# Symmetric normalised adjacency with residual layer norm: four of forty gate products go to GpSimd, and two rows are added at a time

## The reference, cut to what matters

```python
# x: (8, 2048, 64), W = adj: (8, 2048, 2048), U: (2048, 16), all float32
Ws = 0.5 * (W + swapaxes(W, -1, -2))
A = sigmoid(U @ U.T)                      # the gate: symmetric, the same for all batches
K = Ws * A[None]
d = rsqrt(maximum(K.sum(axis=-1), 1e-12))
K = K * d[:, :, None] * d[:, None, :]
x = layernorm(x + w_scale * einsum('bnm,bmc->bnc', K, x))
```

## Time and profile before

| | |
|---|---|
| median of three runs | 469.59 us |
| the profiled execution | 466.65 us |
| its span, first to last instruction | 464.8 us |
| TensorE busy | 436.6 us, 94% |
| VectorE busy | 416.3 us, 90% |
| ScalarE busy | 208.4 us, 45% |
| GpSimd busy | 113.4 us, 24% |
| moved by DMA | 143.11 MB, mean 308 GB/s |
| mean granted TensorE clock | 0.988 |

### The profile page before, as it was taken

How to read it: one execution, slowest core, us unless ns; L and a number is a source line. 1 busy time by engine, 2 the same in 40 slices (tenths; PEclk the granted TensorE clock), 3 DMA queues, 4 the chain that set the end, 5 groups by cost and what they waited for, 6 DMA issues and landing times.

```text
span 464.8 us, 14448 instructions
## 1 busy us (share of the span) xinstructions
PE 436.6 (94%) x5318; PEld 232.5 (50%) x5318; DVE 416.3 (90%) x1154; ACT 208.4 (45%) x655; POOL 113.4 (24%) x133
## 2 busy tenths in 40 slices
PE   7888999999999999989999899989999899999893
PEld 6556444554455543555445544565445543564351
DVE  6988868999899998999899998999899999999645
ACT  3797432554255442554335533463426542554320
POOL 0000000022520334103340235103340225203443
PEclk9997999999999999999999999999999999999998
DMA  8999699988999799997999898998989998994012
GB/s 285 388 327 381 240 383 329 355 314 305 333 365 321 280 364 315 373 339 272 361 336 356 295 362 302 391 335 298 383 308 355 333 328 309 385 334 179 2 45 47
DMA packets 101387, 143.11 MB, mean 308 GB/s; under 512 B 35824, under 2 KB 35824, under 8 KB 101360
## 3 DMA queue, kind: packets, MB, share of 16 engines
q1 hardware_dynamic: 86496, 139.01, 84.4%
q10 hardware_dynamic: 14864, 3.74, 3.7%
HBM read 138.54 MB, written 4.19 MB: 307 GB/s over the span
## 4 chain that ended last, share of the span: by engine, by line
PE 67%; DVE 15%; issue 7%; ACT 5%; DMA 4%; POOL 0%; DVEq 0%; POOLq 0%; ACTq 0%; SPq 0%
PE yp L442 39%; PE kt L400 12%; PE tw L400 11%; DVE k L671 7%; DVE k L682 5%; ACT k L564 3%; DMA k<-in_adj_dram 3%; PE yp L540 3%; ACT gate L551 2%; PE yp L475 1%; DVE z L702 1%; DMA h<-in_L_gnn_U_dram 1%; DVE deg_parts L682 1%; PE kt L486 1%; PE kt L540 0%
## 5 line engine op out<-in xcount | busy, mean ns | idle before, releaser
L564 ACT ACTIVATE k<-kt 128x512 f32<-128x512 f32 (+3 forms) x288 | 149.2, 523 | 213.8 <-PE kt L400 213.7
L442 PE MATMUL yp<-k,z 128*64 128x512 f32 x944 | 233.2, 607 | 4.3 <-DVE z L702 3.9
L671 DVE TENSOR_TENSOR k<-tw,k 128x512 f32<-128x512 f32 (+2 forms) x320 | 193.0, 603 | 19.8 <-PE tw L400 15.7
L682 DVE CUSTOM_DVE_ANT_0 k<-k,gate 128x512 f32<-128x512 f32 (+2 forms) x320 | 198.7, 621 | 0.0
L400 PEld LDWEIGHTS kt<-ident,k 64*128 64x128 f32 x1920 | 74.3, 140 | 93.4 <-issue 74.5
L400 PEld LDWEIGHTS tw<-ident,k 64*128 64x128 f32 x2176 | 82.6, 140 | 43.9 <-issue 38.5
L400 PE MATMUL kt<-ident,k 64*128 64x64 f32 x1920 | 93.9, 231 | 10.6 <-ACT k L564 9.1
L400 PE MATMUL tw<-ident,k 64*128 64x64 f32 x2176 | 99.0, 228 | 1.5 <-DVE k L671 1.0
L442 PEld LDWEIGHTS yp<-k,z 128*64 128x64 f32 x944 | 55.8, 136 | 69.3 <-issue 54.7
L327 POOL TENSOR_TENSOR d<-deg,minus_half 128x4 f32<-128x4 f32 x32 | 32.4, 1014 | 206.8 <-DVE deg L692 206.2
L564 ACT ACTIVATION_READ_ACCUMULATOR k<-kt 128x1 f32 x288 | 57.2, 199 | 0.0
(11 more groups left out here) (53 smaller groups left out, 140.4 us busy)
## 6 DMA issues: line engine op xcount, KB each, us to landing
k<-in_adj_dram SPq DMA_DIRECT2D x128, 1024.0 KB, 7.3
xt<-in_x_dram ACTq DMA_DIRECT2D x7, 512.0 KB, 8.0
out_dram<-h SPq DMA_DIRECT2D x7, 512.0 KB, 8.4
xt<-in_x_dram SPq DMA_DIRECT2D x1, 512.0 KB, 14.0
out_dram<-k SPq DMA_DIRECT2D x2, 128.0 KB, 2.1
out_dram<-k SPq DMA_DIRECT2D x3, 64.0 KB, 1.7
h<-in_L_gnn_U_dram SPq DMA_DIRECT2D x1, 128.0 KB, 3.4
out_dram<-k ACTq DMA_DIRECT2D x1, 64.0 KB, 1.9
```

The lines of the kernel that those rows point to most:

```text
L442: t = pe.matmul(yp[at:at + C, m // 2, :], z[:, n * G + c, :], K[(n, m)][:, c, :], start=(q == first_unit[m] and c == 0), stop=(q == last_u ...
L564: nc.scalar.activation(K[(j, i)][:, r, c0:UW].rearrange("p (c h e) -> p c h e", h=2, e=H), whole_rows(kt[:, 0:2, :], r % 2, (UW - c0) // P ...
L671: nc.vector.tensor_tensor(row, whole_rows(tw[:, tw_bank[g] // 2 * 2:tw_bank[g] // 2 * 2 + 2, :], g % 2, w // P), row, ALU.add).then_inc(su ...
L682: nc.vector.tensor_tensor_reduce(row, row, A[:, A_AT[g]:A_AT[g] + w], 1.0, 0.0, ALU.mult, ALU.add, deg_parts[:, i * G + r, j:j + 1]).then_ ...
```

## The change

GpSimd makes the gate product of rows 3, 12, 22 and 33 (`POOL_ROWS`; three are 512 wide, row 33 is 256 wide) as a plain product without a row sum. ScalarE takes the row sum of each of these four rows by an extra copy into a scrap tile, four rows later in its own list (`SUM_LAG`). VectorE leaves these rows out and makes 36 gate products. In the six steps off the diagonal VectorE adds two rows by one instruction of 1024 elements (`add_two_rows`), so 24 adds become 12. TensorE's upper transposes wait for a second semaphore (`pool_lower_done`), and the degree sums wait for `row_summed`. The load order of the next batch is changed in two places, and the rows at which the later steps stand are moved, most by one to four rows, `COPY_ROWS[0]` by seven.

```diff
-LOADS = [(0, 1), (0, 0), (0, 2), (0, 3), (1, 0), (1, 1), (1, 2), (2, 0), (1, 3), (3, 0), ...]
+LOADS = [(0, 0), (0, 1), (0, 2), (0, 3), (1, 0), (1, 1), (1, 2), (1, 3), (2, 0), (3, 0), ...]
+POOL_ROWS = [3, 12, 22, 33]
+NP, ND = len(POOL_ROWS), NL - len(POOL_ROWS)
+SUM_LAG = 4
-PRODUCT_ROWS = [29, 29, 32, 32, 33, 33, 35, 35, 38, 38, 39, 39, 42, 44, 44, 45, 45, 45, 46, 46, 46, 47, 50, 50, 52, 54, 56, 56, 58, 60, 62, 64]
-DEG_ROWS = [25, 32, 40, 43]
-Z_ROWS = [26, 35, 43, 44]
-KEEP_ROW = 55
-SCALE_ROW = 50
-COPY_ROWS = [55, 65]
-Y_ROWS = [66, 68]
-Y_SCALE_ROWS = [66, 69]
-ADD_ROWS = [68, 69, 69, 73]
-MEAN_ROW = 76
-CENTER_ROWS = [77, 79, 80, 82]
+PRODUCT_ROWS = [30, 30, 32, 32, 33, 33, 35, 35, 38, 38, 39, 39, 42, 44, 44, 45, 45, 45, 45, 47, 47, 47, 50, 50, 52, 54, 56, 56, 59, 59, 61, 63]
+DEG_ROWS = [25, 32, 42, 42]
+Z_ROWS = [26, 34, 42, 43]
+KEEP_ROW = 59
+SCALE_ROW = 47
+COPY_ROWS = [48, 63]
+Y_ROWS = [63, 68]
+Y_SCALE_ROWS = [63, 68]
+ADD_ROWS = [67, 68, 68, 74]
+MEAN_ROW = 75
+CENTER_ROWS = [75, 77, 78, 78]
...
-VAR_ROW = 84
-DIVIDE_ROWS = [87, 89, 91, 94]
+VAR_ROW = 83
+DIVIDE_ROWS = [85, 87, 88, 91]

 # GpSimd
+            def gate_product(b, g, first):
+                s, r = LOWER[g]
+                w = lower_width(s, r)
+                row = K[STEPS[s]][:, r, 0:w]
+                if first:
+                    pool.wait_ge(gate_ready, g + 1)
+                pool.wait_ge(sum_done, b * NL + (g + 1))
+                nc.gpsimd.tensor_tensor(row, row, A[:, A_AT[g]:A_AT[g] + w], ALU.mult).then_inc(pool_lower_done, 1)

 # TensorE, transpose_rows
-                    pe.wait_ge(lower_done, b * NL + G * (s + 1))
+                    pe.wait_ge(lower_done, b * ND + vector_rows_of(G * (s + 1)))
+                    if POOL_ROWS[0] < G * (s + 1):
+                        pe.wait_ge(pool_lower_done, b * NP + pool_rows_of(G * (s + 1)))

 # ScalarE
+            def row_sum(b, g):
+                s, r = LOWER[g]
+                i, j = STEPS[s]
+                w = lower_width(s, r)
+                act.wait_ge(pool_lower_done, b * NP + (POOL_ROWS.index(g) + 1))
+                nc.scalar.activation(scrap[:, 0:w], K[(i, j)][:, r, 0:w], ACT.Copy,
+                                     accum_out=deg_parts[:, i * G + r, j:j + 1]).then_inc(row_summed, 1)
+                    if row - SUM_LAG in POOL_ROWS:
+                        row_sum(b, row - SUM_LAG)

 # VectorE
+            def add_two_rows(b, g):
+                s, r = LOWER[g]
+                rows = K[STEPS[s]][:, r:r + 2, :].rearrange("p r (c h e) -> p (r c) h e", h=2, e=H)
+                if r == 0:
+                    dve.wait_ge(loaded[STEPS[s]], b * 16 + 16)
+                dve.wait_ge(tw_done, b * NL + (g + 2))
+                pair = tw[:, tw_bank[g] // 2 * 2:tw_bank[g] // 2 * 2 + 2, :].rearrange("p h (c e) -> p c h e", e=H)
+                nc.vector.tensor_tensor(rows, pair, rows, ALU.add).then_inc(sum_done, 2)

 # VectorE, sum_degrees
+                dve.wait_ge(row_summed, b * NP + pool_rows_of(G * (top + 1)))

 # VectorE, steps
-                    add_row(b, g)
+                    if STEPS[g // G][0] == STEPS[g // G][1]:
+                        add_row(b, g)
+                    elif g % 2 == 0:
+                        add_two_rows(b, g)
```

More of the change, by code:

```diff
@@ L39 @@
 LAST_PAIR_OF_BANK = [max(q for q, pair in enumerate(PAIRS) if pair[0][1] // 2 == k) for k in range(2)]
-LOADS = [(0, 1), (0, 0), (0, 2), (0, 3), (1, 0), (1, 1), (1, 2), (2, 0), (1, 3), (3, 0), (2, 1), (3, 1), (2, 3), (3, 2), (2, 2), (3, 3)]
+LOADS = [(0, 0), (0, 1), (0, 2), (0, 3), (1, 0), (1, 1), (1, 2), (1, 3), (2, 0), (3, 0), (2, 1), (3, 1), (2, 3), (3, 2), (2, 2), (3, 3)]
 STORE_AFTER = (3, 1)
@@ L60, with pool_rows_of, vector_rows_of @@
 UPPERS_TO = [sum(upper_rows(t) for t in range(s + 1)) for s in range(len(STEPS))]
+POOL_ROWS = [3, 12, 22, 33]
+NP, ND = len(POOL_ROWS), NL - len(POOL_ROWS)
+SUM_LAG = 4
+def pool_rows_of(n):
+    return sum(g < n for g in POOL_ROWS)
+def vector_rows_of(n):
+    return n - pool_rows_of(n)
 A_AT = [sum(lower_width(*g) for g in LOWER[:n]) for n in range(NL + 1)]
 UPPER_LAG = 2
-PRODUCT_ROWS = [29, 29, 32, 32, 33, 33, 35, 35, 38, 38, 39, 39, 42, 44, 44, 45, 45, 45, 46, 46, 46, 47, 50, 50, 52, 54, 56, 56, 58, 60, 62, 64]
-DEG_ROWS = [25, 32, 40, 43]
-Z_ROWS = [26, 35, 43, 44]
-KEEP_ROW = 55
-SCALE_ROW = 50
-COPY_ROWS = [55, 65]
-Y_ROWS = [66, 68]
-Y_SCALE_ROWS = [66, 69]
-ADD_ROWS = [68, 69, 69, 73]
-MEAN_ROW = 76
-CENTER_ROWS = [77, 79, 80, 82]
+PRODUCT_ROWS = [30, 30, 32, 32, 33, 33, 35, 35, 38, 38, 39, 39, 42, 44, 44, 45, 45, 45, 45, 47, 47, 47, 50, 50, 52, 54, 56, 56, 59, 59, 61, 63]
[9 more added lines that the diff above has]
+CENTER_ROWS = [75, 77, 78, 78]
 SQUARE_ROW = 83
-VAR_ROW = 84
-DIVIDE_ROWS = [87, 89, 91, 94]
+VAR_ROW = 83
+DIVIDE_ROWS = [85, 87, 88, 91]
 LN_PARTS = 4
@@ L151, in bass_graph_resnorm_kernel @@
         rstd = sb("rstd", [P, NC])
+        scrap = sb("scrap", [P, UW])
         ws = sb("ws", [P, 1])
@@ L219, in bass_graph_resnorm_kernel @@
         banks_taken = sem("banks_taken")
+        pool_taken, pool_lower_done, row_summed = sem("pool_taken"), sem("pool_lower_done"), sem("row_summed")
         deg_summed, deg_ready, d_ready, z_ready = sem("deg_summed"), sem("deg_ready"), sem("d_ready"), sem("z_ready")
@@ L327, in degrees @@
                 nc.gpsimd.tensor_tensor(d[:, s], deg[:, s], minus_half[:, s], ALU.pow).then_inc(d_ready, 1)
+            def gate_product(b, g, first):
[6 more added lines that the diff above has]
+                nc.gpsimd.tensor_tensor(row, row, A[:, A_AT[g]:A_AT[g] + w], ALU.mult).then_inc(pool_lower_done, 1)
             def beside_row(b, row):
-                pool.wait_ge(lower_done, b * NL + row)
+                pool.wait_ge(lower_done, b * ND + vector_rows_of(row))
             def beside(b, row, lag):
@@ L351, in steps @@
                 for row in range(NL):
+                    if row in POOL_ROWS:
+                        gate_product(b, row, lags == 1)
                     for lag in range(lags - 1, -1, -1):
@@ L683, in gate_product, with gate_row_product @@
                                                deg_parts[:, i * G + r, j:j + 1]).then_inc(lower_done, 1)
+            def gate_row_product(b, g, first):
+                if g not in POOL_ROWS:
+                    gate_product(b, g, first)
             def sum_degrees(b, k):
                 n0, n1, top = Z_GROUPS[k]
-                dve.wait_ge(lower_done, b * NL + G * (top + 1))
+                dve.wait_ge(lower_done, b * ND + vector_rows_of(G * (top + 1)))
+                dve.wait_ge(row_summed, b * NP + pool_rows_of(G * (top + 1)))
                 dve.wait_ge(upper_done, b * NU + UPPERS_TO[top])
@@ L759, in steps @@
                     if g:
-                        gate_product(b, g - 1, lags == 1)
+                        gate_row_product(b, g - 1, lags == 1)
                     elif lags > 1:
-                        gate_product(b - 1, NL - 1, lags == 2)
+                        gate_row_product(b - 1, NL - 1, lags == 2)
                     for lag in range(lags - 1, -1, -1):
@@ L833, in _ @@
                 steps(b, 3)
-            gate_product(B - 1, NL - 1, False)
+            gate_row_product(B - 1, NL - 1, False)
             for k in range(NZ):
```

## The result

The changed kernel takes 474.13 us (median of 20 runs, 472.05 to 478.80) where the kernel before, run beside it, takes 470.37 (20 runs, 465.13 to 476.11). The ratio, made from pairs on the same chip, is 1.0127 [1.0094, 1.0159]: slower by 1.3%, where the forecast was faster by 1.2%. Ratios leave out the executions that ran disturbed, and medians take in all of them (two of these were as long as 594 and 1002 us), so a ratio is not the quotient of two medians. The profiled execution took 473.46 us with a span of 471.3, against 466.65 and 464.8.

The account below looks back on a forecast made before the run. TensorE was taken as the bound, VectorE close behind. Start +0.7, turn one -0.6, turns two and three -1.5 and -2.0, four late turns -2.4 gave -5.8: from 469.6 to 463.8 us, range 454 to 473.

Parts of the forecast that it names:

- rival A: Whole kernel: VectorE is the real pacer and TensorE's modelled ends hide it; 444 to 452 us, chance 0.10.
- D: VectorE's adds: the two-row pattern streams no faster, so the merge does nothing; 465 us, chance counted within the forecast's 0.55.
- Rival C: At row 46: GpSimd's product of row 3 comes late for TensorE's transposes; 472 to 479 us, chance 0.13.
- rival B: At rows 26 to 28: the gain is eaten where x, load (3,2) and z meet; 466 to 469 us, chance 0.22.
- Where the stall goes: Walk of VectorE and TensorE through rows 24 to 30: about 1.25 us of TensorE idle, a turn of 52.2.
- the early turns: Turns two and three, 54.2 us after a late load, were to gain 1.5 and 2.0, down to 52.2.
- Queues passed: Reordered loads: units only fill earlier, (2,0) keeps about 6.5 us, x just fits; cost 0 to 1 us a turn.
- the start: First batch: ScalarE's row sums at rows 7 and 16 delay kt copies; +0.7 us taken, +1.2 at most.
- Four of them cost nothing: ScalarE's four row sums, 0.6 to 0.8 us each, fall into its idle time, except in the first batch.
- Contention: VectorE beside GpSimd: 0.25 us per overlap and no full block; four GpSimd products cost 1.0 us, at most 2.

Follow-up runs that it names:

- product_first: Changed kernel with the last gate product of a step moved ahead of the next step's two-row add: 466.83 us, 0.9953 of the kernel before; run again 0.9994.
- half-load kernels: Only half of each unit loaded from the second batch on: changed kernel 467.59 us, ratio 0.9959; kernel before 466.24 us, ratio 0.9890.
- loads_of_before: Changed kernel with the load order of the kernel before: 476.53 us, 1.0151 of the kernel before.
- pool_only_narrow: Kernel before with the four rows on GpSimd and ScalarE, GpSimd multiplying only 32 columns of each: 473.14 us, ratio 1.0105.
- pool_only_no_sums: Kernel before with the four products on GpSimd but without ScalarE's row sums for them: 467.85 us, ratio 0.9979.
- rows_and_loads_only: Kernel before with the moved rows and new load order only, all gate products on VectorE and single adds: 479.39 us, ratio 1.0227.
- pool_only: Kernel before with only the four rows moved to GpSimd and ScalarE, old lists and single adds: 474.63 us, ratio 1.0105.
- merge_product_first: Kernel before with two-row adds and the last product of a step ahead of them, nothing on GpSimd, old lists: 475.93 us, ratio 1.0142.

## Why the prediction was wrong, by its own steps

The profiled span was forecast to shrink by 5.8 us and grew by 6.5, a miss of 12.3: start 1.75, turn one 0.65, turns two and three 3.75, the four late turns 6.1 (forecast -2.4, measured +3.70), the end 0.05.

**What held.** TensorE bounds the kernel: VectorE lost 17 us of work and the kernel got slower, so rival A is out. TensorE's work of a late turn was forecast at 50.9 and is 50.67. VectorE's is 48.08 (forecast about 48). The group of two-row adds has a mean of 1220 ns (forecast 1.21 us) and starts 1.13 apart from what follows, so the merge is worth 0.08 an add, as taken; D is out. GpSimd's product of 512 took 1.27 to 1.66 us, median 1.65 (1.4 taken). Rival C is out: the product of row 3 ends at 343.96 and TensorE asks for it at 344.77, without waiting. The timelines of GpSimd and TensorE:

```profile
342.68 1.28 POOL L354 TENSOR_TENSOR k<-k,gate 128x512 f32<-128x512 f32 x1
```

```profile
344.77 0.48 PE L429 MATMUL kt<-ident,k 64*128 64x64 f32 x10
```

x was never what a late turn waited for (it landed in 6.2 us, median), and VectorE waited for no load at rows 26 to 28 of one, so rival B's mechanism is not seen where it was put.

The Trainium skill, "VectorE: DVE Perf Modes", section on the TRN2 errata, has the formula (N + 151) / 0.96 ns, an estimate of 1224 ns for 1024 elements, and the trace agrees (1220). Its fixed part is not what a merge saves: that was 0.08 us.

**Step that failed first: "Where the stall goes".** The walk found the right product at kt(26), but with 0.7 us and not 1.17, and gave 1.25 for a turn that has 2.27. Its clock left out the way of a signal from engine to engine, 0.24 us from the end of VectorE's read to the start of TensorE's transposes (369.44 to 369.68), which is half of what is missing there. It was made for rows 24 to 30 alone, though five steps end with the same order on VectorE, the last product behind the first two-row add of the next (rows 11, 15, 19, 23 and 27): at kt(18) that costs 0.58, a place that the walk doesn't reach. And of the two waits of 0.35 on ScalarE that moving the copies of y "removes", one stays. That TensorE waits for this order is shown by product_first: the two waits go, and the turn falls to 52.30. That this is nearly the 52.2 of the forecast is luck in part, since its idle places are not the walk's: 0.90 and 0.35 for ScalarE's copies and 0.22 for z, where the walk had 0.7 and 0.5 for gate products and nothing for ScalarE. The term was wrong by 0.8 us a turn, some 5 to 6 us in all. Before, the same product stood behind an add of 0.60 us, half as long. So the merge doubled the instruction in front of the one that TensorE waits for, against a saving of 0.08. How much of the 1.75 us of waits is the merge's and how much the moved lists', which take TensorE's other work away from these rows, was not separated: no run has the new lists and GpSimd's products with single adds.

**Step that failed second: the early turns, and "Queues passed".** Turns two and three were to fall to 52.2, since VectorE had run without slack after a late load. They did not fall, and late loads came to turn four too. The step gave the order of loads a price of nothing because "(2,0) still has about 6.5" us; (2,0) took 6.0 to 7.3 us in six turns and 8.40 in turn four. The margin was read from one turn of one trace. The half-load kernels show what loads cost the changed kernel: some 8 us by the ratios, 6.3 in the turns of the profiled executions. Restoring the old order does not help (loads_of_before): (2,0) then lands in time and another unit is late.

**Third: the start.** +2.45 us against +0.7, but for another reason: loads_of_before has the same instructions there and takes 44.63. The granted clock was low from 20.4 to 27.2, inside the start, and in the kernel before from 40.9 to 47.8, at its edge. The reason given (ScalarE's row sums decide there) is shown in part, on single executions whose clock was high through the whole start: with the lists of before it took 44.83 with the row sums (pool_only_narrow) and 43.78 without (pool_only_no_sums), but with the new lists 44.62 with them (product_first) and 44.85 without (rows_and_loads_only).

**"Four of them cost nothing".** What ScalarE's row sums cost under the new lists was not measured. With the lists of before they cost 0.9 us a turn (pool_only against pool_only_no_sums), though ScalarE is busy less than half of it: the argument by busy share was wrong.

**Contention: the sum held, the reading of the earlier trace rows did not.** They don't show a toll of 0.25 us but a wait. When a gate product or z, which read both inputs from SBUF, starts while GpSimd runs a product, sum or difference of two SBUF operands, it is longer by what the GpSimd instruction still has to run, less 0.12 to 0.15 us: in 56 such cases in the changed kernel, in 45 in the one before, and in every other trace here. In the earlier trace rows the product at 265.51 found 0.38 us left of GpSimd's two sums and lost 0.25. Timelines of GpSimd and VectorE in the changed kernel:

```profile
72.33 1.27 POOL L354 TENSOR_TENSOR k<-k,gate 128x512 f32<-128x512 f32 x1
```

```profile
72.40 1.49 DVE L757 TENSOR_TENSOR z<-xt,d 128x256 f32<-128x256 f32 x1
```

z takes 0.43 elsewhere. Here 1.20 us were left, and it lost 1.06. In product_first, a product of 0.68 us made 1.16 with 0.61 left:

```profile
306.14 1.66 POOL L354 TENSOR_TENSOR k<-k,gate 128x512 f32<-128x512 f32 x1 [9.71 <-DVE k L712]
```

```profile
307.19 1.16 DVE L732 CUSTOM_DVE_ANT_0 k<-k,gate 128x512 f32<-128x512 f32 x1
```

GpSimd waits in the same way: its product takes 1.28 alone, and 1.66 here, where it starts inside the gate product at 305.98. The adds, which read tw from PSUM, are not stretched (45 cases, within 0.01 us). A late turn has 1.9 us of stretch on VectorE, against 0.9 before: 1.0 more, as forecast, but only 0.4 of it beside GpSimd's gate products; most stands beside its normalising instructions.

The Trainium skill, "SBUF — State Buffer", section "Who interferes with whom", has the pair of ports that VectorE and GpSimd share as an exclusive lock, and the traces agree, up to those last 0.12 to 0.15 us. The prediction's reading against it was wrong.

**What stays open.** Why units land later in one turn than in the next: (1,3), (2,0) and (3,0) all took 2.4 to 2.8 us longer in turn four of the changed kernel than in turn five. Why the low-clock stretch of the first batch falls where it does: the mean granted clock of the changed kernel was 0.980 over 20 executions and of the one before about 0.987, and within each of these two 0.01 of it goes with 2.2 and 2.6 us, so that some 1.5 of the 5 to 6 us between the kernels go with the clock; whether the change lowers it was not shown. And the issue stall: it stands in the first pass of the loop, in all seven kernels that have the new lists with both parts and whole loads (2.1 to 3.2 us); in the others it is 0.9 at most, and in none with half loads is it seen; an instruction packet of queue 8 starts just before it, at 151.6 in the changed kernel. But such packets come every 7 to 17 us up to 169, and rows_and_loads_only has one at 151.6 too and no stall. That code is fetched behind the loads is a guess, and the cause stays open.

## What to carry to other kernels

Merging two small instructions saved 0.08 us each time here, and makes whatever stands behind the first of them late by the length of one: before merging, list for every queue place what stands behind the merged instruction and who waits for it, and let that go first. Walk all places of that kind, not only the one that waits today, and add the time of a signal to each crossing (0.2 us). Busy share says nothing about a queue that another engine waits for: ScalarE was busy less than half of the time, and four more row sums on it still cost 0.9 us a turn with the lists of before. A GpSimd instruction on two SBUF operands is priced at its whole remaining length for a VectorE instruction of that kind beside it. When the engine that bounds the kernel also waits for loads in some turns, take the slack from the slowest landing in the trace and not from one turn, and do not book those turns as gain.

## What the runs showed of the hardware

- A single idle place of TensorE can be followed by some 3.5 us at 1.2 GHz, here within 1.1 us of its end: behind 1.99 us in the changed kernel (247.96, clock low from 249.0), behind 2.09 in loads_of_before (304.75, low from 305.7), behind 1.36 in merge_product_first (low from 313.9). The stall is paid for nearly twice: eight product matmuls took 3.60 us in place of 1.94. It need not follow: behind 2.12 us at 154.23 the clock stayed at 1.00, and the same 1.36 at 369.08 left it there too.
- A VectorE instruction with both inputs in SBUF and a GpSimd product, sum or difference of two SBUF operands hardly overlap: the one that starts second waits for the first, to within 0.12 to 0.15 us of its end (56 cases in the changed kernel, the largest 1.06 us on a z of 0.43). An add that reads PSUM is not held, and nothing was held beside GpSimd's powers: gate products of 512 that started there took 0.69.
- GpSimd multiplies 512 columns in 1.27 us alone and in 1.65, median, in the changed kernel, where it mostly starts inside a gate product.
- The start takes 43.8 to 48.1 us in these kernels, and TensorE's clock is low for 0 to 13.6 us of it.
- A row sum on ScalarE is a copy of 0.63 us, median, and a read of 0.20, and four of them cost a turn of TensorE 0.9 us with the lists of before.
